# Cross attention on one core: the first batch is peeled, its context loaded first, and the weights prepared behind its Gram products

## What is computed

```
g_x     = (g_w @ x_2 + g_b)^T
theta_x = (theta_w @ x + theta_b)^T
phi_x   = phi_w @ x_2 + phi_b
W       = theta_x @ phi_x / N
y       = (W @ g_x)^T
out     = bn_gamma * (w_w @ y + w_b - bn_mean) / sqrt(bn_var + eps) + bn_beta + x
```

## Time and profile before

| | before |
|---|---|
| median of 3 runs | 810.12 us (809.64 to 811.26) |
| profiled execution | 808.35 us |
| its span, first to last instruction | 806.5 us |
| mean granted TensorE clock | 0.992 |
| busy TensorE / VectorE / ACT / GpSimd | 778.9 / 529.1 / 304.4 / 535.9 us |
| TensorE busy in 100 to 150 us | 50.00 of 50 us |
| longest wait of TensorE in the opening | 9.3 us |

### The profile page before, as it was taken

How to read it: one execution, slowest core, us unless ns; L and a number is a source line. 1 busy time by engine, 2 the same in 40 slices (tenths; PEclk the granted TensorE clock), 3 DMA queues, 4 the chain that set the end, 5 groups by cost and what they waited for, 6 DMA issues and landing times.

```text
span 806.5 us, 11687 instructions
## 1 busy us (share of the span) xinstructions
PE 778.9 (97%) x4045; PEld 664.8 (82%) x4045; DVE 529.1 (66%) x901; ACT 304.4 (38%) x508; POOL 535.9 (66%) x351
## 2 busy tenths in 40 slices
PE   4499999999999999999999999999999999999997
PEld 2388888888888888888888888888888888888885
DVE  3858485775848667484875848577584866758254
ACT  2545242533414353342434424243452435334121
POOL 0888577785757868575785857688575777857400
PEclk9799999999999999999999999999999999999999
DMA  8735517163360826427072541717345071640202
GB/s 217 205 107 104 210 28 216 69 172 140 79 233 1 210 101 156 156 62 249 1 208 104 121 191 42 229 41 182 130 95 217 19 212 81 161 152 1 105 1 104
DMA packets 53011, 103.10 MB, mean 128 GB/s; under 512 B 2410, under 2 KB 35844, under 8 KB 52996
## 3 DMA queue, kind: packets, MB, share of 16 engines
q1 hardware_dynamic: 52996, 102.91, 43.6%
HBM read 69.35 MB, written 33.55 MB: 128 GB/s over the span
## 4 chain that ended last, share of the span: by engine, by line
PE 95%; DVE 2%; DMA 2%; SPq 1%; issue 0%; DVEq 0%; ACT 0%
PE wbank L540 57%; PE gbank L540 36%; DMA ctx_sb<-in_ctx_dram 2%; PE wbank L659 1%; DVE ctxT_lo L422 1%; DVE ctxT L386 1%; DVE z_lo L432 0%; SPq L217 0%; SPq L208 0%; DVE wp_lo L439 0%; DVE x_sb L530 0%; DVE wt_lo L439 0%; DVEq L66 0%; ACT ctxT_hi L297 0%; DVE zb_row L435 0%
## 5 line engine op out<-in xcount | busy, mean ns | idle before, releaser
L264 POOL TENSOR_TENSOR ctxT_lo<-ctxT,ctxT_hi 128x512 fp32r<-128x512 f32 x120 | 162.7, 1356 | 195.8 <-ACT ctxT_hi L297 195.8
L272 POOL TENSOR_TENSOR ctx_sum<-ctx_sum,ctxT 128x512 f32<-128x512 f32 x112 | 171.8, 1534 | 0.9 <-POOL ctx_sum L267 0.2
L280 POOL TENSOR_TENSOR x_lo<-x_sb,x_hi 128x1024 fp32r<-128x1024 f32 x64 | 151.8, 2407 | 2.7 <-ACT x_hi L297 2.7
L297 ACT ACTIVATE mt<-wbank 128x512 fp32r<-128x512 f32 x64 | 38.3, 598 | 250.7 <-PE wbank L540 250.7
L454 DVE TENSOR_TENSOR stage<-gbank,mt 128x384 f32<-128x384 f32 x64 | 28.4, 485 | 145.9 <-PE gbank L540 145.9
L530 DVE SCALAR_TENSOR_TENSOR x_sb<-wbank,const,x_sb 128x512 f32<-128x512 f32 x112 | 79.1, 747 | 67.6 <-PE wbank L540 67.6
L540 PE MATMUL wbank<-ctxT_lo,ctxT_hi 128*128 128x512 f32 x512 | 118.7, 389 | 0.0
L297 ACT ACTIVATE ctxT_hi<-ctxT 128x512 fp32r<-128x512 f32 x128 | 79.3, 629 | 102.9 <-DVE ctxT L386 102.9
L540 PEld LDWEIGHTS wbank<-ctxT_lo,ctxT_hi 128*128 128x128 f32 x512 | 95.1, 188 | 18.7
L386 DVE STREAM_TRANSPOSE ctxT<-ctx_sb 128x512 f32<-128x512 f32 x128 | 81.7, 683 | 10.4 <-DMA ctx_sb<-in_ctx_dram 10.4
L540 PE MATMUL wbank<-x_hi,wt_hi 128*128 128x512 f32 x256 | 81.7, 400 | 0.0
(11 more groups left out here) (100 smaller groups left out, 1346.9 us busy)
## 6 DMA issues: line engine op xcount, KB each, us to landing
ctx_sb<-in_ctx_dram SPq DMA_DIRECT2D x64, 512.0 KB, 8.4
x_sb<-in_x_dram SPq DMA_DIRECT2D x16, 2048.0 KB, 7.8
out_dram<-x_sb SPq DMA_DIRECT2D x64, 512.0 KB, 2.6
x_sb<-in_L_xattn_w_w_dram SPq DMA_DIRECT2D x1, 512.0 KB, 3.8
x_sb<-in_L_xattn_g_w_dram SPq DMA_DIRECT2D x1, 512.0 KB, 3.6
phi_nat<-in_L_xattn_phi_w_dram SPq DMA_DIRECT2D x1, 512.0 KB, 13.0
stage<-in_L_xattn_theta_w_dram SPq DMA_DIRECT2D x1, 512.0 KB, 12.7
bp_row<-in_L_xattn_phi_b_dram SPq DMA_DIRECT2D x1, 128.0 KB, 11.7
```

The lines of the kernel that those rows point to most:

```text
L264: nc.gpsimd.tensor_tensor(ctxT_lo[:, c, :], src, f(ctxT_hi[:, c, :]), ALU.subtract).then_inc(ctxT_lo_made, 1)
L272: nc.gpsimd.tensor_tensor(ctx_sum[:, :], ctx_sum[:, :], src, ALU.add).then_inc(ctxT_used, 1)
L280: nc.gpsimd.tensor_tensor(x_lo[:, k, :], x_sb[par][:, k, :], f(x_hi[:, k, :]), ALU.subtract).then_inc(x_lo_made, 1)
L297: nc.scalar.activation(dst, src, ACT.Copy).then_inc(sem_, 1)
```

## The change

The loop keeps its bodies, but batches 0 and 1 run as straight code ahead of it (six loop passes instead of seven). For batch 0:

- Context loads come first, in two halves by columns, partition groups 0 and 1 on SP's queue, 2 and 3 on ACT's, the vectors between the halves, four of them on each queue. Then w, g, theta, phi, x, the phi bias row. Chunks 4 to 7 go to the unused second x buffer, so no chunk waits for the ring.
- VectorE's tiny operations for `scale` and `const` stand between the eight transposes; the last eight (gamma, scale, three for the constant, nbp, two of bg_wide) stand behind the last transpose.
- GpSimd makes all eight low parts, then the sums, then x_lo of blocks 2 and 3.
- TensorE does the high products and the M products of a chunk together, M in four banks. Then it turns w, theta and phi, does the turned blocks, Z and its bias row as three products each, and only then theta(0). The column sums come behind theta(0).
- ACT scales w; w^T, g and g's bias are split like the rest. theta(0) waits until Z is split (`z_taken` 4) and phi and theta too.
- VectorE's `next_ctx` (four transposes of the second context) stands behind the first `low_lo`, the columns of S behind transposes 4 and 5.

```diff
@@ batches
-            with_pairs = (B - 2) // 2
-            with eng.Fori(0, with_pairs) as t:
+            body(0, 0, 0, True, True)
+            body(1, 0, 1, True, True)
+            with eng.Fori(1, B // 2 - 1) as t:
@@ helpers
+        def load_first_ctx(eng, parts, half):
+            src = ctx_in[0].rearrange("(k q) (a n) -> a q k n", q=32, a=QT)
+            cols = slice(half * (QN // 2), (half + 1) * (QN // 2))
+            for a in parts:
+                eng.dma_start(ctx_sb[32 * a:32 * a + 32, :, cols], src[a][:, :, cols]).then_inc(in_first[half], 16)
@@ sync
+            load_first_ctx(sp, (0, 1), 0)
+            load_vectors(sp, range(0, 4))
+            load_first_ctx(sp, (0, 1), 1)
             sp.dma_start(w_nat, w_w.rearrange("(m p) c -> p m c", p=P)).then_inc(in_w1, 16)
...
-            load_ctx(0)
+            sp.dma_start(theta_nat, theta_w.rearrange("(k p) c -> p k c", p=P)).then_inc(in_w4, 16)
             sp.dma_start(phi_nat[:, :, :], phi_w.rearrange("(k p) c -> p k c", p=P)).then_inc(in_w3, 16)
...
             sp.wait_ge(zb_done, 1)
+            sp.wait_ge(first_lo, CH)
+            sp.wait_ge(ctxT_used, CH)
             load_x(1, 1)
@@ gpsimd
-            prep_ctx(0, first=True)
-            prep_x(0, 0)
+            for c in range(CH):
+                pool.wait_ge(ctxT_hi_made, c + 1)
+                lo_part(0, c, first_lo)
+            for c in range(CH):
+                sum_up(0, c)
+            sum_rest(0)
+            for k in (2, 3):
+                pool.wait_ge(x_hi_made, k + 1)
+                nc.gpsimd.tensor_tensor(x_lo[:, k, :], x_sb[0][:, k, :], f(x_hi[:, k, :]),
+                                        ALU.subtract).then_inc(first_x_lo_pool, 1)
@@ scalar
+            load_first_ctx(act, (2, 3), 0)
+            load_vectors(act, range(4, 8))
+            load_first_ctx(act, (2, 3), 1)
...
+            act.wait_ge(scale_made, 1)
+            act.wait_ge(in_w1, 16)
+            for m in range(KC):
+                nc.scalar.activation(w_nat[:, m, :], w_nat[:, m, :], ACT.Identity,
+                                     scale=scale[:, m:m + 1]).then_inc(w_scaled, 1)
+            act.wait_ge(in_w2, 16)
+            hi(g_hi, g_nat, g_hi_made)
+            act.wait_ge(wide_made, KI)
+            hi(bg_hi, bg_wide, bg_hi_made)
...
+            for i in range(KC):
+                act.wait_ge(m_done, min(i + 1, KC - 1))
+                if i == KC - 1:
+                    act.wait_ge(gram_chunk, CH)
+                hi(mt[:, i, :], FIRST_M_BANK[i][:, :], m_made)
+                if i > 1:
+                    act.wait_ge(w_turned, i - 1)
+                    hi(wsT_hi[:, i - 2, :], W_BANK[i - 2][:, :], w_hi_made)
+            for g, dst in enumerate((wt_hi[:, 0:2, :], wt_hi[:, 2:4, :], wp_hi[:, 0:2, :], wp_hi[:, 2:4, :])):
+                act.wait_ge(tp_turned, g + 1)
+                hi(dst, TP_BANK[g][:, :].rearrange("p (k c) -> p k c", k=2), tp_hi_made)
+            act.wait_ge(in_x[0], 16)
+            first_x_hi(0)
+            first_gram_hi(0)
+            first_gram_hi(1)
+            z_hi_part(0)
+            first_gram_hi(2)
+            first_x_hi(1)
+            z_hi_part(1)
+            first_x_hi(2)
+            z_hi_part(2)
+            first_x_hi(3)
+            z_hi_part(3)
@@ vector
+            transpose_chunk(0, 7)
+            chain(nc.vector.tensor_tensor(r0, r2, gamma_, ALU.mult))
+            nc.vector.tensor_scalar(scale[:, :], r0, 1.0 / N, None, ALU.mult).then_inc(scale_made, 1)
             chain(nc.vector.tensor_tensor(wm, wb_, mean_, ALU.subtract))
+            chain(nc.vector.tensor_tensor(r3, wm, r0, ALU.mult))
             chain(nc.vector.tensor_tensor(const[:, :], r3, beta_, ALU.add))
+            chain(nc.vector.tensor_scalar(nbp_col[:, :], bp_col[:, :], float(N), None, ALU.mult))
             dve.wait_ge(ones_done, 1)
             for k in range(KI):
                 nc.vector.tensor_scalar(bg_wide[:, k, :], f(ones_r[:, :]), bg_col[:, k:k + 1], None,
+                                        ALU.mult).then_inc(wide_made, 1)
...
+            dve.wait_ge(g_hi_made, 1)
+            nc.vector.tensor_tensor(g_lo, g_nat, f(g_hi), ALU.subtract).then_inc(g_lo_made, 1)
+            dve.wait_ge(bg_hi_made, 1)
+            nc.vector.tensor_tensor(bg_lo, bg_wide, f(bg_hi), ALU.subtract).then_inc(bg_lo_made, 1)
             for k in range(KI):
+                dve.wait_ge(w_hi_made, k + 1)
+                nc.vector.tensor_tensor(wsT_lo[:, k, :], W_BANK[k][:, :], f(wsT_hi[:, k, :]),
+                                        ALU.subtract).then_inc(w_taken, 1)
...
+            for i in range(len(PLAIN)):
+                gram_sum(0, i)
+            z_lo_part(0)
+            gram_lo_part(0, 0)
+            first_x_lo_part(0)
+            z_lo_part(1)
+            gram_lo_part(0, 1)
+            first_x_lo_part(1)
+            z_lo_part(2)
+            gram_lo_part(0, 2)
+            z_lo_part(3)
             dve.wait_ge(zb_done, 1)
+            nc.vector.tensor_copy(zb_row[:, :], ZB_BANK[:, :]).then_inc(zb_taken, 1)
@@ tensor
+                if first(b):
                     for c in range(CH):
+                        s_chunk(c)
+                        pe.wait_ge(first_lo, c + 1)
+                        for i in range(KC):
+                            ins = mm(FIRST_M_BANK[i][:, :], hi_of(c, i), ctxT_lo[:, c, :], c == 0, c == CH - 1)
...
+                if first(b):
+                    turn_w()
+                    turn_theta_phi()
...
+                        if k == 0 and m == 0 and first(b):
+                            pe.wait_ge(tp_taken, 4)
+                            pe.wait_ge(z_taken, 4)
...
+                if first(b):
+                    make_z()
                 theta(0, (0, 1))
+                if first(b):
+                    pe.wait_ge(z_taken, 2)
...
                 theta(0, (2, 3))
+                if first(b):
+                    pe.wait_ge(zb_taken, 1)
+                    column_sums()
```

More of the change, by code:

```diff
@@ L380, in chain, with transpose_chunk @@
                 dve.wait_ge(vec_step, steps[0])
[L382 to L386 removed]
+            def transpose_chunk(b, c):
+                if not first(b):
+                    if isinstance(b, int) and b == 1 and c < RING:
+                        dve.wait_ge(ctxT_used, c + 1)
+                    else:
+                        dve.wait_ge(ctxT_used, CH * b + (c + 1 - RING))
+                nc.vector.transpose(turned_ctx(b, c).rearrange("p (k q) -> p k q", q=32),
@@ new lines, in gram_lo_part, with first_x_lo_part @@
+            def gram_lo_part(b, i):
+                a, z = BANK_SPAN[i]
+                dve.wait_ge(gram_hi_made, 3 * b + (i + 1))
+                nc.vector.tensor_tensor(gram_lo[:, a:z], stage[:, a:z], f(gram_hi[:, a:z]),
+                                        ALU.subtract).then_inc(gram_lo_made, 1)
+            def first_x_lo_part(k):
+                dve.wait_ge(x_hi_made, k + 1)
+                nc.vector.tensor_tensor(x_lo[:, k, :], x_sb[0][:, k, :], f(x_hi[:, k, :]),
+                                        ALU.subtract).then_inc(first_x_lo, 1)
@@ L458, in body @@
-                for i, (a, z) in enumerate(BANK_SPAN):
-                    dve.wait_ge(gram_hi_made, 3 * b + (i + 1))
-                    nc.vector.tensor_tensor(gram_lo[:, a:z], stage[:, a:z], f(gram_hi[:, a:z]),
-                                            ALU.subtract).then_inc(gram_lo_made, 1)
+                        transpose_chunk(b + 1, c)
+                if not first(b):
+                    if nxt:
+                        next_ctx()
+                    for i in range(len(PLAIN)):
+                        gram_sum(b, i)
+                    for i in range(len(BANK_SPAN)):
+                        gram_lo_part(b, i)
@@ L561, in setup @@
+                        ins = mm(Z_BANK[j][:, :], g_lo[:, k, cols], wsT_hi[:, k, :], False, k == KI - 1)
+                    ins.then_inc(z_done, 1)
+                pe.wait_ge(tp_taken, 4)
+                pe.wait_ge(bg_lo_made, 1)
                 for k in range(KI):
-                    ins = nc.tensor.matmul(gbank[0][:, :], bg_wide[:, k, :], wsT[:, k, :], start=k == 0,
-                                           stop=k == KI - 1)
+                    mm(ZB_BANK[:, :], bg_hi[:, k, :], wsT_hi[:, k, :], k == 0, False)
+                    mm(ZB_BANK[:, :], bg_hi[:, k, :], wsT_lo[:, k, :], False, False)
+                    ins = mm(ZB_BANK[:, :], bg_lo[:, k, :], wsT_hi[:, k, :], False, k == KI - 1)
@@ L577, in _ @@
[L577 to L579 removed]
+            turn_vectors()
             pe.wait_ge(ident_r_made, 1)
```

369 lines of the change are left out of this document (207 added, 162 removed).

## The result

| | before | after |
|---|---|---|
| median | 810.21 us (4 runs, 809.64 to 811.26) | 804.39 us (4 runs, 803.30 to 806.09) |
| ratio | 1 | 0.9929, 95% interval 0.9905 to 0.9952 |
| profiled execution, its span | 808.35, 806.5 us | 806.09, 804.3 us |
| granted clock in it | 0.992 | 0.991 |
| second batch's first products | 85.66 us | 84.48 us |

The change gains 0.7%, 5.8 us by the medians. Between the two profiled executions the difference is 2.3 us, and between the marks at the second batch 1.2 us. These three numbers don't agree, and a good part of what the forecast missed lies in why.

The account below looks back on a forecast made before the run. TensorE's steady work bounds the kernel, so only the opening counts: a 27 us lead after M is given back by weights' work, waits, idle and cold start, mark +0.3 us, hence 810.5 us; range 804.3 to 813.5.

Parts of the forecast that it names:

- where the lead goes: After M, a 27 us lead spent: weights' work 9.8, TensorE's waits 6.6, idle 7.7, cold start 1.8, t wait 1.7.
- the t wait: TensorE, after three t blocks, stands 1.7 us because VectorE transposes the next context ahead of theta's low halves.
- VectorE's waits for GpSimd's two x_lo: In VectorE's chain before theta(0): 4.1 us of waits for two GpSimd operations of 2.4 us each.
- rival (ii): Context load: 512-byte packets take the time of 1 KB ones, halves land 5 and 10 us later; 815 to 820, chance 0.13.
- (iii): Context load: two queues reach about 280 GB/s, halves at 6.8 and 10.4 us; 809.2 with port waits, within the 0.52.
- step (b): VectorE's eight tiny operations after the last transpose each wait up to 1.45 us for GpSimd; wide_made at 27.3 us.
- The mark of 86.0: Forecast start of the second batch's products, against 85.66 before; the shift of 0.3 us was added to the median.
- the cold start: At theta(0): TensorE restarts at a lower clock after its idle time, costing 1.8 us.
- what the lead pays: Its item for TensorE's waits between M and Z: 33.2 - 23.1 less 2.9 transposes and 0.8 turned blocks, given as 6.6.
- rival (i): VectorE's tiny operations do not wait for GpSimd, or only two-tensor ones do: 805.6 or 806.8 us, chance 0.28.
- rival (iii) with rival (i): Faster context load and tiny operations not waiting together: mark -5.9 us, 804.3 us, the range's lower edge.
- t_block(3) within 1 us of 62: Sign that the forecast is right: the fourth t block starts at 62.1 us, against 62.0 before.

Follow-up runs that it names:

- the second profile: The kernel before, unchanged, run and profiled once more: median 810.03 us, second batch's mark at 87.57 us.
- the filled kernel: Under the base of the sum: the kernel before with unread products in TensorE's 9.3 and 2.3 us waits, 808.45 us. Under the cold start: the filled one.
- both reorders: Changed kernel with Z's halves ahead of most of the Gram matrix's and the second context's four transposes ahead of low_lo: 797.52 us, ratio 0.9856.
- Z's halves first: Changed kernel with ScalarE and VectorE making Z's halves ahead of most of the Gram matrix's: 798.75 us, ratio 0.9878.
- the filled one: Changed kernel with thirty unread products in TensorE's wait between Z's bias row and theta(0): 803.36 us, ratio 0.9915.

## Why the prediction was wrong

The forecast was 810.5 us, no change; the kernel takes 804.4, at the lower edge of the range given. In the terms of the sum:

- **Right: where the lead goes.** M at 23.1 us (measured 23.4); TensorE idle before theta(0) for 7.7 us (7.2); the t wait of 1.7 us (1.7); VectorE's waits for GpSimd's two x_lo 4.1 us (2.0 in the gram_lo of 2.73, which takes 0.73 without, and 2.1 in the x_lo of 3.35). The first half landed at 7.5 us instead of 8.0, the second at 13.5 instead of 13.2: rival (ii), slow packets of 512 bytes, is out, and (iii), a faster load, came in by half its measure for the first half and not for the second.
- **Wrong in size, the step that failed: the tiny operations, step (b).** The sum had all but one of their seven intervals wait for a whole GpSimd instruction, bg_wide ready at 27.3 us; it was ready at 24.1. The mechanism is the one forecast (1.22 and 1.33 us against 0.16 with GpSimd standing). But not each of them waited in full: from 17.44 us on, their rows show 0.58, 1.22, 1.33, 0.52, 0.16, 1.15 and two in 1.58 us. Beside GpSimd's rows (low parts of 1.27 us each up to 20.5, a copy up to 21.07, sums of 1.35 each from 21.15) every one that waited ends within 0.1 us of where an instruction of GpSimd ends. The first began in the middle of one and the fourth fell on the short copy; the fifth, 0.16 us, and the last, 0.27, slipped in where GpSimd was between two. So four of the eight waited for a whole long instruction, and not six of seven intervals. The Trainium skill's SBUF — State Buffer, "Who interferes with whom", has the later of the two engines blocked until the other's instruction ends; the trace agrees, with these ends. The last transpose was also 0.8 us earlier. From there all of the chain on VectorE stands 3.2 to 3.5 us earlier, theta(0) at 44.2 instead of 47.7. This is 3.2 us of the miss, the lower clock included: by an estimate from the profiles' terms a median of 804.39 is a mark of about 82.8 (time less 1.8 outside the span less 719.8 from mark to end), and 86.0 was forecast.
- **Wrong: the base of the sum.** The mark of 86.0 was set against 85.66 in the profiled execution, and the difference of 0.3 us was added to the median, 1.8 us above that execution. But 85.66 isn't the mark of the median: by the same estimate (810.12 less 1.8 less 720.8) that is about 87.5, and the second profile has 87.57. Added to the profiled execution's own terms, a mark at 86.0 gives 808.7. The experiment with the filled kernel shows what most of the 1.8 us are: the median of before falls by 1.4 us when TensorE has something to do in its long wait.
- **Not foreseen: the end.** The forecast took all behind the second batch's mark for the same in both kernels. From the mark to the end of the span it is 720.8 us before (806.5 - 85.66; 720.6 in the second run) and 719.8 after (804.3 - 84.48; 719.9). The steady work is the same to 0.2 us; the difference stands behind the last operation of VectorE, 4.2 us before the end in one kernel and 3.1 in the other. All eleven profiles of the changed kernel and its variants have the short end (3.0 to 3.1), the second profile of before and the filled kernel before the long one (4.0 and 4.1). The last load of code shows in the DMA queues of this stretch, 804 to 806 us, of before (packets, MB, share):

```profile
q14 instruction: 1, 0.01, 1.0%
```

All three profiles with the long end have this packet in their last 3 us, and none of those with the short one has. That the engines wait for it is argued from this, not shown.
- **Right on average, but not fixed: the cold start.** 1.8 us were taken for theta(0). Its first twelve products took 5.3 us in the profile of the result (44.20 to the transposes at 49.46) and 4.2 in the second one (44.23 to 48.43), where 12 x 0.23 = 2.8 at full pace: 2.5 and 1.4 us. A second fall, behind the t wait, was not in the sum. It stands in the profile of the result and in that of the filled kernel, and in none of the five others with a wait of 1.7 to 1.8 us there.
- **A slip in the list of what the lead pays:** 33.2 less 23.1, 2.9 and 0.8 is 6.4, not 6.6. The mark doesn't rest on it.

Together: 3.2 for VectorE's chain (the lower clock within it), 1.8 for the base, 1.0 for the end make the 6 us between 810.5 and 804.4.

The chances named 0.28 for the tiny operations not waiting, 805.6 to 806.8 us. The time came out below even that, though they did wait in part, since base and end lie outside all cases: no case had put the reference itself in doubt. That it lies within 0.1 us of the 804.3 of rival (iii) with rival (i), the lower edge of the range, is luck: the second half of the context came no faster than forecast, and the tiny operations did wait. The sign "t_block(3) within 1 us of 62" failed: it started at 59.60 and 58.48.

## What to carry over

Where a kernel has a long wait of TensorE in its opening, one profiled execution fixes neither the clock behind it nor the mark of the first steady work: compare absolute times within one execution, and look at a second one before a difference is added to a median. Work moved ahead of a chain on VectorE is worth what VectorE's queue lets through: here two reorders of split operations, with no work saved, gave 6.5 us, more than the whole change (5.8). Filling TensorE's waits gained 1.4 us in the kernel before, and in the changed one, where a second wait of 1.8 us stayed, nothing that the intervals tell from none. Count VectorE's waits for GpSimd by laying the two engines' rows beside each other, not for each operation in full.

## What the runs showed of the hardware

- TensorE's granted clock fell to 0.50 during or behind the wait in each profile with one of 5.6 to 7.2 us ahead of theta(0), and in both of the kernel before, with 8.6 and 9.3 us ahead of phi's transposes. With a wait of 2.9 us ahead of theta(0) it fell in one profile (both reorders, at 42 us) and not in another (Z's halves first, 1.00 from 38 to 66). With one of 1.7 to 1.8 us ahead of the last t block it fell in two (after, the filled one) and not in five. Behind a wait of 1.15 us at the very start it fell too, though 28 matmul records had run just before.
- An operation of VectorE on 128 x 4 elements takes 0.16 us alone and up to 1.33 us beside GpSimd, and ends within 0.1 us of where GpSimd's instruction ends; GpSimd's x_lo of 2.5 us beside it makes VectorE's of 1.2 us last 3.35.
- The first context's 512-byte runs to 32-partition groups first moved at 330 to 352 GB/s and then mostly at 200 to 240, on one queue as on two (with some stretches up to 300 on two).
